# Adaptive-norm attention and a six-layer local-attention stack on one core: barrier taken out, token shift moved from matrix products into copies and a DMA, inverse root in nine steps, new orders on every engine

## The reference

```
h  = layernorm(x) * (1 + scale_c) + shift_c            # scale, shift, gates from silu(c) @ wmod
x1 = x + gate1 * causal_attention(h)                   # 8 heads of 128, rotary
xr = layernorm(x1) * (1 + scale2_c) + shift2_c
for l in range(6):                                     # the stack
    s  = shift_tokens(xr)      # channels 64..127 of each token come from the token before, 0 for the first
    q, k, v = split(s @ Wqkv[l])                       # 16 heads of 64
    q, k = rotate(l2norm(q) * qs), rotate(l2norm(k) * ks)
    xr = xr + window_attention(q, k, v) @ Wo[l]        # windows of 32, each looks at itself and the one before
    y  = layernorm(shift_tokens(xr)) * g + b
    a, gate = split(y @ W1[l] + b1[l])                 # 341 + 341 columns
    xr = xr + (a * gelu(gate)) @ W2[l] + b2[l]
out = x1 + gate2 * xr
```

## Time and profile before

| | |
|---|---|
| median of 3 runs | 1872.15 us (1868.36 to 1875.66) |
| the profiled execution: its own time / its span | 1868.75 us / 1867.0 us |
| busy share of the span | PE 93%, PEld 77%, DVE 79%, POOL 79%, ACT 75% |
| granted TensorE clock, mean | 0.983 of full speed |
| first stage, barrier at its end | 0 to about 276 us |
| stack | about 278 us to the end |

### The profile page before, as it was taken

One profiled execution on the slowest core, in us unless ns is written; L12 is line 12 of the kernel. 1 busy time (PEld: TensorE's weight loads), 2 busy tenths in 40 slices (PEclk: granted clock), 3 DMA queues, 4 the chain that ended last, 5 costly groups with the idle time before them and its releaser, 6 DMA issues. The chain is left out here.

```text
span 1867.0 us, 66200 instructions
## 1 busy us (share of the span) xinstructions
PE 1732.8 (93%) x26984; PEld 1428.9 (77%) x26985; DVE 1472.2 (79%) x2952; ACT 1404.0 (75%) x2772; POOL 1479.4 (79%) x1830
## 2 busy tenths in 40 slices
PE   6999967899999999999999999999999999999985
PEld 4788755777778888787887787877778877888773
DVE  5878847778977888888879787888888798889752
ACT  3777744678877888878877877888788878788862
POOL 3777757779888887988888879789888888898860
PEclk9999988999999999999999999999999999999998
DMA  4000011111121111111110211112111101110100
GB/s 140 1 1 1 1 36 34 31 44 32 31 68 44 33 43 32 58 44 42 44 32 22 68 44 43 31 33 67 40 37 44 32 22 41 38 50 22 37 27 23
DMA packets 45485, 70.67 MB, mean 38 GB/s; under 512 B 15476, under 2 KB 28928, under 8 KB 45184
## 3 DMA queue, kind: packets, MB, share of 16 engines
q1 hardware_dynamic: 43712, 64.34, 11.8%
q10 hardware_dynamic: 1472, 2.10, 0.3%
HBM read 21.33 MB, written 1.05 MB: 12 GB/s over the span
## 5 line engine op out<-in xcount | busy, mean ns | idle before, releaser
L1087 POOL TENSOR_TENSOR ra<-ra,rb 128x512 f32<-128x512 f32 x384 | 492.3, 1288 | 116.7 <-DVE rb L1083 111.6
L1132 POOL TENSOR_TENSOR qn<-ra,rs 128x512 f32<-128x512 f32 x384 | 401.3, 1058 | 7.2 <-POOL rs L1125 0.8
L1062 DVE TENSOR_REDUCE ss<-sq 128x8 f32<-128x512 f32 x384 | 260.4, 678 | 91.2 <-ACT sq L1051 91.2
L1214 POOL TENSOR_TENSOR sp<-sp,rl 128x512 f32<-128x512 f32 x192 | 200.0, 1046 | 61.7 <-DVE rl L1209 61.0
L1201 ACT ACTIVATE sp<-sp 128x512 f32<-128x512 f32 x192 | 121.7, 634 | 38.5 <-DVE sp L1196 38.1
L1205 DVE TENSOR_REDUCE sm<-sp 128x8 f32<-128x512 f32 x192 | 128.6, 670 | 15.5 <-ACT sp L1201 13.0
L1179 PE MATMUL pP<-kT,qT 64*32 64x64 f32 x4608 | 106.9, 226 | 2.8 <-issue 2.2
L1179 PEld LDWEIGHTS pP<-kT,qT 64*32 64x32 f32 x4608 | 93.8, 105 | 16.3 <-ACT kT L1152 11.0
L489 POOL TENSOR_TENSOR ra<-ra,rb 128x512 f32<-128x512 f32 x64 | 81.5, 1288 | 29.6 <-DVE rb L485 29.6
L1190 DVE TENSOR_REDUCE mx<-pS 128x8 f32<-128x512 f32 x48 | 32.9, 685 | 91.2 <-PE pP L1179 91.2
L1083 DVE TENSOR_TENSOR rb<-pQ,rope 128x512 f32<-128x512 f32 x144 | 97.9, 680 | 2.9 <-POOL ra L1087 2.9
(11 more groups left out here) (355 smaller groups left out, 6194.3 us busy)
## 6 DMA issues: line engine op xcount, KB each, us to landing
vs<-v SPq DMA_DIRECT2D x96, 384.0 KB, 3.3
wqkvA<-in_L_ffn_Wqkv SPq DMA_DIRECT2D x18, 512.0 KB, 5.6
vs<-v SPq DMA_DIRECT2D x96, 64.0 KB, 3.0
woB<-in_L_ffn_Wo SPq DMA_DIRECT2D x6, 512.0 KB, 4.2
w<-in_L_ffn_W SPq DMA_DIRECT2D x6, 341.0 KB, 2.9
out<-x SPq DMA_DIRECT2D x4, 256.0 KB, 2.3
x<-in_L_attn_x SPq DMA_DIRECT2D x1, 768.0 KB, 8.1
w<-in_L_ffn_W SPq DMA_DIRECT2D x12, 64.0 KB
```

Source lines behind the costliest of these rows:

```text
L1062: e.tensor_reduce(ss[:, j, :], sq[:, j % 2, :].rearrange("p (h d) -> p h d", d=DB), AX.X, ALU.add).then_inc(b_ss.sem, 1)
L1087: e.tensor_tensor(ra[:, j, :], ra[:, j, :], rb[:, j % 2, :], ALU.add).then_inc(b_ad.sem, 1)
L1132: e.tensor_tensor(qn[:, j % 4, :].rearrange("p (h d) -> p h d", d=DB), ra[:, j, :].rearrange("p (h d) -> p h d", d=DB), rs[:, c % 2, 8 * j ...
L1214: e.tensor_tensor(y, y, rl[:, u, :].unsqueeze(2).to_broadcast([P, 8, 64]), ALU.mult).then_inc(b_pn.sem, 1)
```

## The change

- **Join.** `barrier` and `mark_written` are gone. The last two calls of `first_attention` and the first call of the stack (layer 0, pair 0) are replaced by `join_pe`, `join_act`, `join_dve`, `join_pool`, written-out orders in which the end of sequence 7 and the chunks 0 and 1 of layer 0 are mixed. `scaled_rope(e, 0)` moves into the first stage (sequence 3), the memset of `gT` to the first `gated(.., 2)`.
- **Shift in copies.** `xt_turn` is two plain transposes of 128 x 128; `xt_high` and `xt_low` each become two instructions, one for each 64 partitions, the second one column further on.
- **Shift in one DMA.** `l_shift` moves from PE to SP: a DMA of 127 partitions by 2 KB (`fx[1:P] <- xr[0:P-1]`) and one of two pieces of 256 bytes. SP waits for `out_add` and for the `l_norm` before. `l_second` is gone; `l_first` moves from POOL to ACT, behind the DMA.
- **Root in nine steps.** Steps 0 to 4 on POOL, 5 to 8 on DVE. Steps 5 to 8 are `scalar_tensor_tensor` with two SBUF inputs of 128 x 64.
- **FFN earlier.** `l_root` and `l_norm` stand in the call of `p - 1`, no longer in that of `p - 2`.
- **`finish`** of a pair stands inside the last layer and the remainder, two pairs after the pair (`DONE = 2`).
- **Orders and banks.** All four written-out orders and all bank lists are new, found by a search that assumes a longer time from one engine to another; the loads of weights stand at other places of SP's order.

The core of the diff (the new join functions and the orders are cut):

```diff
-        def barrier(e, n):
-            e.drain().then_inc(e_bar.sem, 1)
-            e.wait_ge(e_bar.sem, (n + 1) * 4)
-            e.sem_inc(e_hold.sem, 1)
...
-            lo, hi = slice(0, HALF), slice(HALF, M)
-            xc = xr[:, (c % B) * NT:(c % B + 1) * NT, :]
+            if l == 0:
+                e.wait_ge(a_x.sem, a_x.at(c, 1))
             for t in range(NT):
-                e.matmul(o[lo, t * P:(t + 1) * P], xc[:, t, lo], ident, start=True, stop=True)
-            e.matmul(o[hi, 0:P], xc[:, 0, hi], down, start=True, stop=True)
-            e.matmul(o[hi, P:T], xc[:, 1, hi], down, start=True, stop=False, skip_group_check=True)
-            e.matmul(o[hi, P:T], xc[:, 0, hi], wrap, start=False, stop=True, skip_group_check=True)\
-             .then_inc(b_xt.sem, 1)
+                i = flip(e, o, t, xr[:, (c % B) * NT + t, :])
+            i.then_inc(b_xt.sem, 1)
+
+        def shifted(l, c, x_):
+
+            o = xt_bank(l, c)
+            return ((x_[0:HALF, c % 2, :], o[0:HALF, 0:T]), (x_[HALF:M, c % 2, 1:T], o[HALF:M, 0:T - 1]))
...
-            e.copy(xsh[:, c % 2, :], banks[XT_BANK[c % 2]][:, 0:T]).then_inc(b_xh.sem, 1)
+            for dst, o in shifted(l, c, xsh):
+                i = e.copy(dst, o)
+            i.then_inc(b_xh.sem, 1)
...
-            e.tensor_tensor(xsl[:, c % 2, :], banks[XT_BANK[c % 2]][:, 0:T], xsh[:, c % 2, :].bitcast(F32),
-                            ALU.subtract).then_inc(b_xs.sem, 1)
+            for (dst, o), (h, _) in zip(shifted(l, c, xsl), shifted(l, c, xsh)):
+                i = e.tensor_tensor(dst, o, h.bitcast(F32), ALU.subtract)
+            i.then_inc(b_xs.sem, 1)
...
+            elif n == FIT:
+                e.scalar_tensor_tensor(p, t, HORNER[0], t, ALU.add, ALU.mult).then_inc(b_rs.sem, 1)
+            elif n < NORM - 1:
+                e.scalar_tensor_tensor(p, p, HORNER[n - FIT], t, ALU.add, ALU.mult).then_inc(b_rs.sem, 1)
             else:
                 e.wait_ge(b_qn.sem, b_qn.at(it - 2, QK - 1))
-                e.tensor_tensor(rs[:, c % 2, :], t, y, ALU.mult).then_inc(b_rs.sem, 1)
+                e.scalar_tensor_tensor(rs[:, c % 2, :], p, HORNER[n - FIT], y, ALU.add, ALU.mult).then_inc(b_rs.sem, 1)
...
+            e.dma_start(fx[0:1, 1::NT, HALF:M], xr[P - 1:P, k:k + FT:NT, HALF:M]).then_inc(f_xs.sem, 16)
+            e.dma_start(fx[1:P, :, :], xr[0:P - 1, k:k + FT, :]).then_inc(f_xs.sem, 16)
+
+        def l_first(e, l, q):
             it = l * FP + q
-            e.wait_ge(f_sh.sem, f_sh.at(it))
-            e.wait_ge(f_ln.sem, f_ln.at(it - 1))
-            e.copy(fx[:, :, HALF:M], banks[SHIFT_BANK][:, 0:FT * HALF].rearrange("p (t m) -> p t m", m=HALF))\
-             .then_inc(f_xs.sem, 1)
+            e.wait_ge(b_wx.sem, b_wx.at(l * B + 2 * q + 1))
+            e.wait_ge(f_xs.sem, f_xs.at(it))
+            e.copy(fx[:, :, 0:HALF], xr[:, tiles(q), 0:HALF]).then_inc(f_xa.sem, 1)
```

More of the change, by code:

```diff
@@ L1152, in turn_copy @@
             e.copy(dst, w.rearrange("p (h q) -> p h q", h=4)).then_inc(b_tc.sem, 1)
-        def mark_written(e):
-            for n in SCORE_BANKS:
-                e.matmul(banks[n], ident16[:, :], maskB[:, :], start=True, stop=True)
         def mask(e, l, c, u):
@@ new lines, in pair_pe @@
+            if on(p - 1):
+                out_proj(e, l, c - 2, 0)
+                out_proj(e, l, c - 2, 1)
+                e.wait_ge(b_sub.sem, b_sub.at(l * B + c - 1, 2))
+            if on(p) and not on(p - 1) and not on(p - 1):
+                e.wait_ge(b_ab.sem, b_ab.at(l * B + c, 2))
+            if on(p):
+                turn(e, l, c, 0)
+            if on(p - 1):
+                e.wait_ge(b_sub.sem, b_sub.at(l * B + c - 1, 3))
+            if on(p) and not on(p - 1):
+                e.wait_ge(b_ab.sem, b_ab.at(l * B + c, 5))
@@ new lines, in pair_pe @@
+            if on(p):
+                proj(e, l, c + 1, 1)
+            if on(p - 2):
+                e.wait_ge(f_G.sem, f_G.at(l * FP + p - 2, 1))
+            if on(p) and on(p - 1) and not on(p - 2):
+                e.wait_ge(b_tc.sem, b_tc.at(l * B + c - 1, 7))
+            if on(p) and not on(p - 2) and not on(p - 1):
+                e.wait_ge(b_ab.sem, b_ab.at(l * B + c, 4))
+            if on(p):
+                turn(e, l, c, 1)
+                e.wait_ge(b_tc.sem, b_tc.at(l * B + c, 0))
+                turn(e, l, c, 2)
@@ new lines, in pair_pe @@
+            if on(p - 1):
+                out_proj(e, l, c - 1, 1)
+            if on(p):
+                scores(e, l, c, 1)
+            if on(p - 2):
+                e.wait_ge(f_G.sem, f_G.at(l * FP + p - 2, 2))
+                second_layer(e, l, p - 2, 0)
+            if on(p - 1):
+                e.wait_ge(b_wx.sem, b_wx.at(l * B + c - 1, 0))
+            if on(p) and not on(p - 1):
+                e.wait_ge(b_ab.sem, b_ab.at(l * B + c + 1, 4))
+            if on(p):
+                turn_p(e, l, c, 1)
@@ L1721, in pair_act @@
                 square(e, l, c + 1, 2)
+                turn_copy(e, l, c, 3)
+                e.wait_ge(b_tc.sem, b_tc.at(l * B + c, 3))
+                mask(e, l, c, 1)
+            if on(p) and last(p):
+                split_high(e, l + 1, 0, 1)
+            if on(p - 1):
+                copy_p(e, l, c - 1, 2)
+            if on(p):
+                square(e, l, c + 1, 3)
+            if on(p - 1):
+                copy_p(e, l, c - 1, 3)
+            if on(p):
+                exponent(e, l, c, 0)
             if on(p - 1):
@@ L1812, in pair_dve @@
                 rotate_sin(e, l, c, 2)
+                square_sum(e, l, c, 3)
+                rotate_cos(e, l, c, 3)
+                rotate_sin(e, l, c, 3)
+                xt_low(e, l, c + 1)
+                square_sum(e, l, c, 4)
+                rotate_cos(e, l, c, 4)
+                rotate_sin(e, l, c, 4)
+                square_sum(e, l, c, 5)
+                rotate_cos(e, l, c, 5)
+                rotate_sin(e, l, c, 5)
+                square_sum(e, l, c, 6)
+                rotate_cos(e, l, c, 6)
+                rotate_sin(e, l, c, 6)
+                square_sum(e, l, c, 7)
+            if on(p - 2):
+                gated(e, l, p - 2, 0)
             if on(p - 1):
@@ L1819, in pair_dve @@
             if on(p):
-                rotate_cos(e, l, c, 3)
+                norm_step(e, l, c, 5)
+                rotate_sin(e, l, c, 7)
+                norm_step(e, l, c, 6)
             if on(p - 1):
@@ L1870, in pair_dve @@
             if on(p):
-                rotate_cos(e, l, c + 1, 1)
-                rotate_sin(e, l, c + 1, 1)
                 square_sum(e, l, c + 1, 2)
@@ L2021, in pair_pool, with stream @@
                 soft_norm(e, l, c, 3)
-        def stream(e, pair):
-            for p in range(FP):
+                normalise(e, l, c + 1, 4)
+            if on(p - 1):
+                l_root(e, l, p - 1)
+            if on(p):
+                normalise(e, l, c + 1, 5)
+        def stream(e, pair, after=lambda p: None):
+            for p in range(1, FP):
                 pair(e, 0, p, lambda q: q >= 0)
```

1128 lines of the change are left out of this document (750 added, 378 removed).

## The result

The changed kernel takes 2086.2 us (median of 4 runs, 2084.9 to 2091.3) against 1871.4 us for the kernel before on the same chip (1868.4 to 1875.7): ratio 1.115, 95% interval 1.112 to 1.118. Forecast were 1815 us and 1780 to 1852, with 0.06 for slower. The profiled execution has a span of 2083.9 us.

The account below looks back on a forecast made before the run. The prediction took PE to bound the stack, but not the seam and the end; 1867.0 - 43 + 16 - 26 - 4 = 1810 us of span, so a median of 1815 us, range 1780 to 1852.

Parts of the forecast that it names:

- term B: Load added to the other engines in the stack, mainly DVE's four root steps: 16 of 43 us given back.
- the bound of 24 us: Shift DMA before l_first: if the cover were 1 us short, ACT stands still 1 us a pair, at most 24.
- Term A: PE's work in the 24 pairs: two-transpose xt_turn saves 25 us, l_shift off PE 18, together 43.
- the prediction's own sign: Stack layers: the forecast is wrong if PE's idle time in a layer grows beyond 15 us.
- rival 1: Stack: DVE's root steps wait fully for POOL and DVE becomes the bound; median 1858 us, chance 0.10.
- Rival 3: Root's relay POOL to DVE to POOL holds each chunk up; 2 us a chunk adds 96, 1911 us; chance 0.06.
- Term C: Seam between first stage and stack: the join shortens it to 85 us, gain 26, bounds 10 and 36.
- Rival 4: Seam: join does nothing, chunk 0 waits behind sequence 7 on POOL; gain 10, median 1831, at the 0.50 range's edge.
- Term D: End of the kernel: finish saves 3.9 us, DMA shift costs 3.5, earlier norm gains 3.5; net 4 us.
- The orders: New orders and banks could close some of PE's 7.9 us a layer or open as much; taken at nothing.

Follow-up runs that it names:

- e1: The changed kernel with the token shift's DMA of 127 rows issued as two, 112 and 15 rows: 1882.4 us, ratio 1.0045 to the kernel before.
- f2: e1 with xt_turn put back to its five products and single copies in xt_high and xt_low, in the new orders: 1869.4 us, ratio 1.000.
- h1: The kernel before with only xt_high and xt_low cut into two instructions each over 64 partitions: 1909.1 us, ratio 1.019.
- f4: e1 with the join taken back (sequence 7 drains, barrier, marking products, pair 0 from nothing): 1894.7 us, ratio 1.011.
- h2: The kernel before with only finish moved earlier, so that one of four is left behind the last add: 1872.9 us, ratio 1.000.
- p3: e1 with 128 increments of an unused semaphore ahead of TensorE's first wait: 1886.2 us, ratio 1.009.
- b4: The kernel before, own orders, banks and barrier, with transposes and shifted copies, shift by cut DMAs and nine-step root: 1939.6 us, ratio 1.037.
- b2: The kernel before, own orders and banks, with only the second token shift by cut DMAs and l_first on ACT: 1925.4 us, ratio 1.029.

## Why the prediction was wrong, step by step

**The step that failed** stands in term B: "landing is 3.0 to 3.3 us after the issue", and from it "I cost this at nothing inside the stack". These rows are of transfers over 96 and 32 rows. The one added has 127 rows and landed after 13.5 us. The cover was sized rightly: in the pair shown, ACT reached `l_first` at 1039.96, 6.6 us behind the start of `out_add` at 1033.33, which is also the median of the 24, and 6.6 had been forecast. The path was right too, `move_v` and the turn copies behind it. But the bound of 24 us let the landing vary by 1 us, when its number of engines had not been looked at: 24 x 8.4 = 202 us.

**Term A** (43 us): the work fell as forecast, its worth did not. In e1 the layer of the earlier trace rows and its plain and dear pair are:

```profile
842.98:1099.49 256.51, 240.21 (x4176) 197.45 (x4176) 223.22 (x430) 207.43 (x387) 203.36 (x219) 1.00 0.16 46
842.98:905.60 62.62, 59.64 (x1044) 49.59 (x1044) 54.26 (x107) 51.10 (x96) 49.76 (x55) 1.00 0.16 45
969.66:1036.09 66.43, 60.84 (x1046) 49.12 (x1044) 59.82 (x111) 53.91 (x102) 52.57 (x56) 1.00 0.12 34
```

TensorE's work: 59.6 a plain pair (forecast 59.1), 6.1 us less a layer (forecast 7.2). Its idle time: 16.3 a layer instead of 8, so the layer is 2 us longer. "Worth its full size only as long as PE stays the bound" was the right condition, and an engine that is busy 97% of a layer did not meet it: with 6 us taken away it waited 8 us more, for code, for DVE and for POOL (the table above). By the prediction's own sign, idle time over 15 us a layer, it was wrong in e1 as well. f2 shows it directly: with the 25 us of work put back the kernel is no slower, and its stack takes as long.

**Term B** (16 us given back, by DVE's four steps): in e1 they take 0.96, 0.22, 0.51 and 0.23 us on average, 1.9 a chunk for 3.2 forecast. Only step 5 mostly waits (median 1.04, least 0.22): 42 of 48 take over 0.8 us, and each ends 0.08 us after an instruction of POOL, an addition in 19 cases but `soft_norm`, which the prediction did not name, in 23. DVE's work in the dear pair is 59.8, not 62.4, and TensorE has more in both kinds of pair, so DVE bounds neither and rival 1 fell. The added copies, costed at nothing, are not free: 36 us in the old orders (h1). Rival 3's mechanism is there, TensorE waiting 17 us for POOL in e1, but far from its 96 us.

**Term C** (26 us, bounds 10 and 36): 12 us between f4 and e1, and pair 1 begins at 345.4 in f4 and at 333.7 in e1. In the changed kernel the first `xt_high` comes at 261.1 instead of 280.0 and POOL's first addition of the stack at 268.7, with sequence 7 still under way, so the join does what it says. But the stretch up to pair 1 keeps a reduced clock (0.80 in e1 from 280 us on), and pair 0 takes 73 us there instead of 61, which gives most of the head start of 19 us back. Rival 4 had the size right, but not the reason: chunk 0 did not wait in line behind sequence 7.

**Term D** (4 us): the 3.9 for `finish` are read in h2, and the changed kernel too has one behind the last add. The shift on the path took 3.6 us in e1 from its first issue (1843.80) to the copy (1847.42), near the forecast. But the end as a whole did not gain: from the start of the last pair to the end of the span e1 takes 138.8 us, the kernel before 128.6, with a granted clock of 0.56 in the last 31 us (0.73 in the kernel before). p3, the same kernel with increments, takes 130.1, so these 10 us are not firm.

**The orders** (taken at nothing): 57 us between b4 and e1, 12 of them the join. They fit the parts, and the parts need them to come out even.

**Still open**: why shorter work on TensorE in the old orders costs a second 34 us beyond h1. Its gaps are waits for code by the traces, but h1, with TensorE's program unchanged, also has 9 us more of them than the kernel before, and increments ahead of the program moved no kernel by more than some 10 us beyond the later start. So the place of the code alone does not explain it. Nothing was run in which packets come earlier.

## What to carry to other kernels

Before a transfer is priced by another's row, compare its row count with that row's: 127 rows went over one DMA engine and landed after 13.5 us, 112 + 15 after 2.9. A microsecond off the busiest engine is a microsecond off the time only if nothing in its order arrives just in time; here an engine busy for 97% of a layer gave none of 37 us back (6.1 a layer). So judge an order together with its parts. And before instructions that "do nothing" are used as a probe, look in the trace for what they delay: 128 increments took 20 us, and 15 of them were time of the kernel. What they left beyond that, some 10 us (0.5%) either way, is the spread to give a small edit of such a kernel before reading a cause into it.

## What the runs showed that was not expected

- One DMA engine moved 25 GB/s in whole rows of 2 KB and some 15 GB/s in pieces of 256 bytes.
- TensorE's code comes in packets of 16 KB, and gaps of up to 6.3 us (in b2) stood inside bursts with no semaphore between. They end 1.1 to 1.6 us after such a packet is through. After one of 2.95 us the granted clock was 0.50 for 6 us.
- An increment of a semaphore took TensorE 0.15 us.
- A `scalar_tensor_tensor` of DVE with two SBUF inputs of 64 columns took 0.21 us alone and up to 1.27 beside POOL's additions or its `soft_norm`, and then ended 0.08 us behind them.
